# Fusion kernel: patch tiles cut across images, chunks of 384 tokens, patch rows normalised in PSUM, three periods

## Chip, core and metric

One core of one Trainium2 chip runs the whole program. The metric is the device time of one execution in microseconds (us). TensorE is called PE here and in the rows, VectorE DVE, ScalarE ACT, GpSimd POOL, and SyncE SP; SP does no arithmetic, it issues every DMA of this kernel.

## What is computed

64 images of 3 x 224 x 224 are cut into 14 x 14 patches of 16 x 16 pixels. Each patch is a row of 768 numbers that is normalised, multiplied into 256 columns and normalised again. 77 text rows are put behind the 196 patch rows of an image, so that an image has 273 tokens. An attention and a gated feed-forward layer follow, each with a residual.

```python
B, C, H, Wd = img.shape
x = img.reshape(B, C, H // PH, PH, Wd // PW, PW)
x = jnp.transpose(x, (0, 2, 4, 3, 5, 1))
x = x.reshape(B, -1, PH * PW * C)
x = _layernorm(x, ln1_g, ln1_b)
x = jnp.einsum('bnd,de->bne', x, W) + b
x = _layernorm(x, ln2_g, ln2_b)
...
h = jnp.concatenate([h, txt], axis=1)
h = h + _L0_attn_ref(_layernorm(h, axis=-1), L0_attn_Wq, L0_attn_bq, L0_attn_Wk, L0_attn_bk, L0_attn_Wv, L0_attn_bv, L0_attn_Wo, L0_attn_bo)
h = h + _L0_ffn_ref(_layernorm(h, axis=-1), L0_ffn_W_r, L0_ffn_W_k, L0_ffn_W_v, L0_ffn_mu_r, L0_ffn_mu_k)
...
return y.reshape(n, s, h, d).transpose(0, 2, 1, 3)
...
scores = jnp.einsum('nqhd,nkhd->nhqk', Q, K) * scale
attn = jax.nn.softmax(scores, axis=-1)
out = jnp.einsum('nhql,nlhd->nqhd', attn, V)
...
xr = mu_r * x + (1.0 - mu_r) * x_prev
xk = mu_k * x + (1.0 - mu_k) * x_prev
r = jax.nn.sigmoid(jnp.einsum('btc,dc->btd', xr, W_r))
k = jnp.einsum('btc,dc->btd', xk, W_k)
k_act = jnp.square(jax.nn.relu(k))
out = r * jnp.einsum('btc,dc->btd', k_act, W_v)
```

Because of the transpose ahead of it, the attention is one among the 16 heads of a single token: 16 x 16 scores for each token, and no token sees another.

## The kernel before, in words

The work has two grains. An **image** is loaded in two DMAs into xim (84 rows: two halves of a patch, three channels, 14 grid rows), copied by ACT into xcols so that a patch column lies together, transposed by PE in 14 pieces (the jobs x, L1106), and split from PSUM into a rounded part (xh, ACT, L951) and the rest (xl, DVE, L770), both in xT. PE multiplies xT by wtok in two halves of 98 rows with 18 matmuls of 258 columns each (the jobs tok, L1118). Column sums of squares (sq on ACT, ssq on DVE L765) go through two small matmuls against imask (the job stat, L1125) in a bank of their own. DVE then takes each half out of PSUM into y (yn, L786), and normalises it in SBUF: bn_stats and bn_aggr, hg (L800: y minus mean times g2b), h (L806: times rs2 plus b2b, into yh). POOL computes the two inverse roots with pow (L625, L609). SP copies yh into hc, which holds the token rows.

A **chunk** is 364 tokens, three to four images ("a quad"), so 48 chunks; its token tiles have 126, 126 and 112 rows. Per chunk: normalise (xn), transpose (xt, L1134), six products of 384 columns (qkv, L1026), a round trip through DRAM (qkv_dram) that brings q and k into qk and v into vrow, spreading of q (qplace, DVE L829) and of k (kspread, four ACT operations of 768 columns, L921) into block-diagonal operands, then scores (s, L1075), softmax, transposes (pt, L1083), the product with v (av, L1096), a second round trip (o_dram), ont (L1152), wo, normalise, zt (L1166), the mix with the token before (mix on DVE L872, mixh on ACT L1000, mixl on POOL L667), and the products k, r and val with their readers kr and rt (ACT, L1005, L1014) and rv (DVE, L878). DRAM rows 364 to 384 of a chunk are zeros, since attention handles 384 rows whatever is in them.

Everything is unrolled, and each engine runs its instructions in the order of one table, AT, of start steps, in which an image recurs every 3000 steps and a chunk every 4000, and all of it every 12000 (a quad):

```python
SLOT, IMG, QUAD = 4000, 3000, 12000
BANK = dict(x=[5, 7, 2], tok=[7, 2], stat=[5], xt=[6, 5], qkv=[4, 1, 6, 3, 4, 3], s=[0, 1], pt=[1, 4], av=[1, 6],
    ont=[1, 3], wo=[3, 6, 5], zt=[1, 6], k=[4, 0], r=[3, 6, 4], val=[0, 1, 3])
```

BANK says which of the eight PSUM banks a PE job writes. Before a job PE waits (turn) until the reader of the bank's last job is done. Every wait of SP stands in the one queue in which all its DMAs stand (helpers after, L284). Each product has six matmuls (three pairings of rounded part and rest, two halves of the depth), all counted under L1026.

Of the kernel before, what the change touches and what calls it, by code (L numbers as in the profile page):

```python
# [10 lines left out]

# [35 lines left out]
VROW = 5 * HD  # L50
# [1158 lines left out]
```

How the kernel before makes its waits and increments, by code:

```python
    def wait(self, eng, q, k, steps):  # L162
        eng.wait_ge(self.sem, q * (self.count * self.per) + (self.base + k * self.per + steps * self.unit))
# [1 line left out]
    def done(self, ins):  # L165
        ins.then_inc(self.sem, self.unit)
        return ins
# [9 lines left out]
    def wait(self, eng, q, k):  # L177
        back, i = divmod(k, len(self.pers))
        eng.wait_ge(self.sems[i], q * self.pers[i] + (2 + back) * self.pers[i] + self.pers[i])
# [267 lines left out]
            def load_rest():  # L448
# [4 lines left out]
                        sp.dma_start(dst, v.rearrange("(a e) -> a e", a=1).broadcast_to((128, E))).then_inc(raw_in, 16)  # L453
                    for n, w in enumerate(WEIGHTS):
                        sp.dma_start(rawsq[n], w.rearrange("(a p) e -> p a e", p=128)).then_inc(raw_in, 16)
                    for s, v in ((0, mu_k), (1, mu_r)):
                        sp.dma_start(mus[:, s, :], v.rearrange("(k p) -> p k", p=128)).then_inc(raw_in, 16)
                sp.wait_ge(prep_pool, 1)
                for c in range(CPQ):
                    sp.dma_start(qkv_dram[c, CT:CTP, :, :].rearrange("t i j -> t (i j)"), qkvt[0:CTP - CT, 0, :]).then_inc(raw_in, 16)
# [9 lines left out]
            def body(q):  # L470
# [10 lines left out]
                    for k in due(q, s, "txt", 0):  # L481
                        back, m = divmod(k, IPQ)
                        c = back * CPQ + text_pieces(m)[-1][2]
                        if q * IPQ + k == 0:
                            sp.wait_ge(prep_act, ACT_CLEAR)
                        after(xn_sb, q, c - CPQ, 3)
                        after(hb_sb, q, c - CPQ, 1)
```

## Time and profile before

| | |
|---|---|
| median of 3 runs | 1630.25 us (1625.87 to 1648.1) |
| profiled execution, first to last instruction | 1635.7 us |
| its mean granted PE clock | 0.968 of full speed |
| busy: PE, DVE, ACT, POOL | 1454.6, 1332.3, 1099.9, 973.6 us |
| DMA packets, bytes | 702658, 227.65 MB |

The page gives no other time for the profiled execution than its span. Busy time counts arithmetic only; SP's share is read from its own queue's rows below.

### The profile page before, as it was taken

What the parts mean: (1) busy time and instruction counts of PE and PEld (TensorE: products, weight loads), DVE (VectorE), ACT (ScalarE), POOL (GpSimd) and SP (SyncE); (2) the same over time, 40 slices, a digit from 0 to 9 for tenths busy, and PEclk for the clock granted to TensorE, in tenths of its full rate; (3) what the DMA queues carried; (4) which work ended last, traced back from release to release, by engine and by line L of the source; (5) the groups of instructions that cost most, each with busy time, mean ns of one, the idle gap of its engine ahead of it and who ended that gap; (6) DMA issues with size and microseconds to landing.
All of it is one profiled execution on the core that took longest, in us unless ns stands there. A gap on an engine that the chain in (4) does not pass through costs nothing. (4 is left out here: it accounts for less than half of the span.)

```text
span 1635.7 us, 53680 instructions
## 1 busy us (share of the span) xinstructions
PE 1454.6 (89%) x18762; PEld 1382.2 (85%) x18762; DVE 1332.3 (81%) x3075; ACT 1099.9 (67%) x2230; POOL 973.6 (60%) x1507
## 2 busy tenths in 40 slices
PE   4678899899999999999999999999999999998856
PEld 4677898898998898889898898998988988897756
DVE  5576888798988989898898888898898988888642
ACT  4455777677777776776777676777777776775543
POOL 2121566567656666666766765675675676576556
PEclk8798999999999999999999999999999999999988
DMA  4279979889877887888887896898898799887651
GB/s 121 59 141 138 141 147 150 125 159 157 143 157 141 147 155 143 150 137 165 149 140 157 151 141 127 167 157 141 152 154 140 151 159 140 156 151 118 131 74 37
DMA packets 702658, 227.65 MB, mean 139 GB/s; under 512 B 617470, under 2 KB 673854, under 8 KB 702394
## 3 DMA queue, kind: packets, MB, share of 16 engines
q1 hardware_dynamic: 702394, 224.23, 77.9%
q8 instruction: 153, 2.51, 0.8%
q14 instruction: 111, 0.91, 0.2%
HBM read 121.64 MB, written 89.64 MB: 129 GB/s over the span
## 5 line engine op out<-in xcount | busy, mean ns | idle before, releaser
L1026 PE MATMUL bank<-wqkv,xnT 128*126 128x384 f32 (+1 forms) x1728 | 354.2, 349 | 5.5 <-issue 5.5
L1118 PE MATMUL bank<-wtok,xT 128*98 128x258 f32 x2304 | 310.2, 290 | 12.0 <-DVE xT L770 11.4
L1026 PEld LDWEIGHTS bank<-wqkv,xnT 128*126 128x126 f32 (+1 forms) x1728 | 294.0, 185 | 18.3 <-issue 10.2
L1118 PEld LDWEIGHTS bank<-wtok,xT 128*98 128x98 f32 x2304 | 294.2, 171 | 14.6 <-DVE xT L770 13.2
L667 POOL TENSOR_TENSOR mixp<-mixf,mixp 128x364 fp32r<-128x364 f32 x192 | 185.2, 976 | 107.2 <-ACT mixp L1000 106.6
L921 ACT ACTIVATE arena<-qk,ymask 128x768 f32<-128x768 f32 x192 | 164.0, 926 | 97.6 <-DMA qk<-qkv_dram 97.6
L843 DVE TENSOR_TENSOR qkvt<-bank,bqkv 126x384 f32<-126x384 f32 (+1 forms) x288 | 154.0, 548 | 48.5 <-PE bank L1026 47.0
L654 POOL TENSOR_TENSOR dT<-zT 128x364 f32<-128x364 f32 x96 | 79.7, 851 | 153.9 <-ACT zT L994 153.9
L609 POOL TENSOR_TENSOR rs<-ve,small 126x3 f32<-126x3 f32 (+1 forms) x160 | 150.3, 940 | 12.5
L607 POOL TENSOR_TENSOR ve<-mv,small 126x3 f32<-126x3 f32 (+1 forms) x160 | 58.8, 368 | 158.8 <-DVE mv L865 104.0
L765 DVE TENSOR_REDUCE xs<-xim 84x14 f32<-84x1792 f32 x64 | 128.7, 2011 | 23.1 <-ACT xim L955 22.8
L872 DVE SCALAR_TENSOR_TENSOR mixf<-dT,mus,zT 128x364 f32<-128x364 f32 x192 | 125.8, 676 | 22.4 <-POOL zT L661 19.5
L943 ACT ACTIVATE xcols<-xim 84x640 f32<-84x640 f32 (+1 forms) x192 | 126.1, 693 | 25.4 <-DMA xim<-in_x 24.1
L1026 PE MATMUL bank<-woT,onT 128*126 128x256 f32 (+1 forms) x864 | 121.9, 287 | 12.4 <-DVE onT L849 12.1
L951 ACT ACTIVATE xT<-bank 128x420 fp32r<-128x420 f32 (+1 forms) x192 | 99.9, 532 | 44.5 <-PE bank L1106 44.2
L1026 PE MATMUL bank<-wrT,mixp 128*126 128x256 f32 (+1 forms) x864 | 124.9, 292 | 4.2 <-POOL mixp L667 3.7
L1026 PEld LDWEIGHTS bank<-woT,onT 128*126 128x126 f32 (+1 forms) x864 | 110.6, 186 | 17.7 <-DVE onT L849 16.9
L1026 PE MATMUL bank<-mixp,wkfT 128*128 128x364 f32 x576 | 123.5, 352 | 1.5 <-POOL mixp L667 1.4
L1075 PE MATMUL bank<-arena,qx 128*32 128x64 f32 x4608 | 83.0, 225 | 43.8 <-issue 43.8
L933 ACT ACTIVATE pt<-bank 64x384 f32<-64x384 f32 x192 | 93.0, 484 | 37.9 <-PE bank L1083 34.5
L682 POOL TENSOR_TENSOR h<-h,r 126x256 f32<-126x256 f32 x144 | 114.2, 807 | 6.1 <-DVE r L878 6.1
L1075 PEld LDWEIGHTS bank<-arena,qx 128*32 128x32 f32 x4608 | 74.1, 112 | 51.1 <-issue 47.4
(121 smaller groups left out, 3339.6 us busy)
## 6 DMA issues: line engine op xcount, KB each, us to landing
xim<-in_x SPq DMA_DIRECT2D x128, 294.0 KB
qk<-qkv_dram SPq DMA_DIRECT2D x48, 768.0 KB, 8.3
qkv_dram<-qkvt SPq DMA_DIRECT2D x96, 378.0 KB
arena<-qkv_dram SPq DMA_DIRECT2D x384, 48.0 KB, 3.9
qkv_dram<-qkvt SPq DMA_DIRECT2D x48, 336.0 KB
o_dram<-probs SPq DMA_DIRECT2D x288, 48.0 KB, 1.9
out<-h SPq DMA_DIRECT2D x96, 126.0 KB
on<-o_dram SPq DMA_DIRECT2D x64, 126.0 KB
```

The source lines that it names most:

```text
L609: done.done(P.tensor_tensor(rs[:, :], ve[:, :], powt[0:part, 0:ve.shape[1]], ALU.pow))
L667: mix_lo.done(P.tensor_tensor(mixp[:, w, 1, kk, :], mixf[:, kk, :], mixp[:, w, 0, kk, :].bitcast(F32), ALU.subtract))
L682: out_sb.done(P.tensor_tensor(dst, dst, r[0:rows, i, :], ALU.add))
L765: x_stats.done(V.tensor_reduce(xs[:, :], xim[:, :].rearrange("p (w q) -> p w q", q=128), AX.X, ALU.add))
L843: qkv_sb.done(V.tensor_tensor(qkvt[0:rows, i, NQ * half:NQ * half + NQ], place("qkv", job)[0:rows, 0:NQ], bqkv[0:rows, :, :].rearrange("p ...
L872: mix_sb.done(V.scalar_tensor_tensor(out=mixf[:, kk, :], in0=dT[:, kk, :], scalar=mus[:, w, kk:kk + 1], in1=zT[:, kk, 0:CT], op0=ALU.mult, ...
L921: kb_sb.done(A.activation(kb[:, :, yy, :], qk[:, :, HD:2 * HD], ACT.Copy, scale=ymask[:, yy:yy + 1]))
L943: x_cols.done(A.activation(xcols[:, 128 * w0:128 * w1].rearrange("p (w r q) -> p w r q", r=HALF, q=PS), xim[:, :].rearrange("p (r w q) -> ...
L951: x_hi.done(A.activation(xT[:, 0, :, w0:w1], src, ACT.Copy))
L1026: ins = mm(psum, left(a, k), right(b, k), start=t == 0, stop=t == len(terms) - 1)
L1075: ins = mm(place("s", part)[32 * j:32 * j + 32, col:col + 64], qx[:, g, :, :].rearrange("p x q -> p (x q)"), kb[:, g, :, :].rearrange("p y ...
L1118: ins = mm(place("tok", c)[0:PT, 0:E + 2], xT[:, a, i0:i0 + GRID // 2, :].rearrange("p i w -> p (i w)"), wtok[:, b, ch, :], start=t == 0, ...
```

## The change

- **Patch tiles.** The 896 grid rows of all images are one sequence, cut every 9 grid rows into 100 tiles of 126 patches. xT becomes a ring of 27 grid rows, so an image's 14 rows may wrap and are then written in two pieces (31 of 64 images: 95 pieces in all). A tile's matmuls are 18 as before. The matmuls on imask go into columns 258 to 271 of the tile's own bank, one set for each image that the tile touches (156 in all), and come ahead of the 18; stat is no job of its own any more.
- **Normalising in PSUM.** yn, hg and h read the tile's bank, yn and hg write back into it, and only h writes SBUF (yh, two buffers). The bank is held until h is done. tok takes banks 7 and 2 in turn, and x takes 5 and 0.
- **Chunks of 384 tokens** in three full tiles of 128 rows, 46 chunks for 17472 tokens; o_dram is a ring of eight images.
- **Attention in halves.** kb and qx hold half a chunk; kspread is two sets of four ACT operations, qplace two sets of two DVE copies, and the scores' second half waits for the second set, which waits for the first half's scores.
- **Mix.** It reads z from PSUM (the zt banks, held until mix is done). zT and d feed POOL as before; the row at an image's start is set by one POOL copy instead of a copy and a memset, with mu less 1 as the factor.
- **sq** writes into xcols in place, so the next xcols waits for ssq, and the next image's load waits only for xcols.
- **Three periods** in a new table: a chunk every 5376 steps, an image every 3822, a tile every 2457, and new banks for the rest.

The core of the diff:

```diff
-IPQ, CPQ = 4, 3
-QUADS = IMAGES // IPQ
-CHUNKS = QUADS * CPQ
-CT = IPQ * T // CPQ
-TOK = [(0, 126), (126, 126), (252, 112)]
-PT = 98
+TOKENS = IMAGES * T
+TT, TILES = 128, 3
+CT = TT * TILES
+CHUNKS = -(-TOKENS // CT)
+TROWS = 9
+PT = TROWS * GRID
+PTILES = -(-IMAGES * GRID // TROWS)
+RING = 3 * TROWS
...
-SLOT, IMG, QUAD = 4000, 3000, 12000
+SLOT = 5376
+IMG = SLOT * T // CT
+PTP = IMG * PT // PATCHES
...
+BANK = dict(x=[5, 0, 5], tok=[7, 2], xt=[3, 4], qkv=[6, 1, 6, 3, 3, 4], s=[3, 1], pt=[4, 1], av=[4, 6], ont=[3, 1], wo=[1, 3,
+    4], zt=[1, 6], k=[4, 6], r=[3, 4, 4], val=[3, 3, 4])
...
+                    y = place("tok", 0, t)[0:pr, 0:E]
...
+                    hg.done(V.scalar_tensor_tensor(out=y, in0=y, scalar=mv2[0:pr, 0:1], in1=g2b[0:pr, :], op0=ALU.subtract, op1=ALU.mult))
...
+                        mix_sb.done(V.scalar_tensor_tensor(out=mixf[:, kk, :], in0=dT[:, kk, :], scalar=mus[:, w, kk:kk + 1],
+                                                           in1=place("zt", kk, k)[:, 0:CT], op0=ALU.mult, op1=ALU.add))
...
+                        for k in due(s, "kspread", 4 * part + yy):
...
+                                qk_in.wait(act, k, 1)
+                                s_pe.wait(act, k - 1 + part, 1 if part else PARTS)
...
+                for t in due(s, "tok", 0):
+                    pr = patch_rows(t)
+                    m = patch_images(t)[-1]
+                    x_stats.wait(pe, m, 1)
+                    turn("tok", 0, t)
+                    for m in patch_images(t):
+                        i0 = TROWS * t - GRID * m + PAD
+                        mm(place("tok", 0, t)[0:pr, E + 2:E + 2 + GRID],
+                           imask[:, :, :].rearrange("p i w -> p (i w)")[:, GRID * i0:GRID * i0 + pr],
+                           xs[:, m % 2, :], start=m == patch_images(t)[0], stop=m == patch_images(t)[-1])
...
+                    terms = [(a, b, ch) for ch in range(KCH) for a, b in ((0, 0), (0, 1), (1, 0))]
+                    for n, (a, b, ch) in enumerate(terms):
+                        ins = mm(place("tok", 0, t)[0:pr, 0:E + 2], xT[:, a, ch, :, :].rearrange("p i w -> p (i w)")[:, r0:r0 + pr],
+                                 wtok[:, b, ch, :], start=n == 0, stop=n == len(terms) - 1)
```

Three places in the order of instructions. **PE, products r and val of one chunk, mid-program.** Here bank0 to bank7 are the PSUM banks, wrT marks an r product, wvfT a val product, wkfT a k product, wtok a patch tile. Before:

```order
L1118 MATMUL bank7<-wtok,xT 98x258 x18
L1026 MATMUL bank3<-wrT,mixp 126x256 x6
L1026 MATMUL bank6<-wrT,mixp 126x256 x6
L1118 MATMUL bank2<-wtok,xT 98x258 x18
L1026 MATMUL bank4<-wrT,mixp 112x256 x6
L1026 MATMUL bank0<-wvfT,kaT 126x256 x6
L1125 MATMUL bank5<-xs,imask 98x14 x2
L1026 MATMUL bank1<-wvfT,kaT 126x256 x6
L1026 MATMUL bank3<-wvfT,kaT 112x256 x6
```

Now, in the changed kernel, where L998 is the product helper and L1102 the tile:

```order
L998 MATMUL bank3<-wrT,mixp 128x256 x6
L1083 MATMUL bank5<-ident,xcols 128x84 x5
L998 MATMUL bank4<-wrT,mixp 128x256 x6
L998 MATMUL bank3<-wvfT,kaT 128x256 x6
L998 MATMUL bank4<-wrT,mixp 128x256 x6
L998 MATMUL bank3<-wvfT,kaT 128x256 x6
L1093 MATMUL bank7<-xs,imask 126x14 x2
L1102 MATMUL bank7<-wtok,xT 126x258 x18
L998 MATMUL bank4<-wvfT,kaT 128x256 x6
L1127 MATMUL bank3<-ident,on 128x128 x3
L1127 MATMUL bank1<-ident,on 128x128 x3
L998 MATMUL bank4<-mixp,wkfT 128x384 x6
```

Six products used five banks (3, 6, 4, 0, 1, 3); now they use two (3, 4, 3, 4, 3, 4) and are interleaved, and the next jobs, ont (ident,on) and k, take the same two banks.

**PE, scores and softmax of one chunk.** arena,qx marks scores, ident,probs the transposes pt, arena,pt2 the product with v. Before:

```order
L1026 MATMUL bank5<-woT,onT 112x256 x6
L1075 MATMUL bank0<-arena,qx 32x64 x24
L1075 MATMUL bank1<-arena,qx 32x64 x24
L1026 MATMUL bank6<-wqkv,xnT 126x384 x6
L1106 MATMUL bank5<-ident,xcols 128x84 x5
L1083 MATMUL bank1<-ident,probs 128x128 x3
L1083 MATMUL bank4<-ident,probs 128x128 x3
```

Now:

```order
L1051 MATMUL bank3<-arena,qx 32x64 x24
L998 MATMUL bank4<-woT,onT 128x256 x6
L1093 MATMUL bank2<-xs,imask 126x14 x2
L1102 MATMUL bank2<-wtok,xT 126x258 x18
L998 MATMUL bank6<-wqkv,xnT 128x384 x6
L1051 MATMUL bank1<-arena,qx 32x64 x24
L1059 MATMUL bank4<-ident,probs 128x128 x3
L998 MATMUL bank3<-wqkv,xnT 128x384 x6
```

The two halves of the scores stood side by side and now have one wo product and one qkv product (in some chunks a tile as well) between them.

**DVE, the patch rows.** bn marks the statistics, g2b marks hg, b2b marks h, bqkv the reader of a qkv product. Before:

```order
L741 TENSOR_REDUCE mx<-bank 128x24
L800 SCALAR_TENSOR_TENSOR y<-y,mv,g2b 98x256
L865 BN_AGGR mv<-bn 126x2
L741 TENSOR_REDUCE mx<-bank 128x24
L746 TENSOR_TENSOR probs<-bank,mx 128x384 x2
L860 BN_STATS bn<-h 112x6
L800 SCALAR_TENSOR_TENSOR y<-y,mv,g2b 98x256
L865 BN_AGGR mv<-bn 112x2
L806 SCALAR_TENSOR_TENSOR yh<-y,rs,b2b 98x256 x2
```

Now:

```order
L766 SCALAR_TENSOR_TENSOR bank<-bank,rstd,c0b 126x256
L770 BN_STATS bn<-bank 126x6
L817 TENSOR_TENSOR qkvt<-bank,bqkv 128x384
L776 BN_AGGR mv<-bn 126x2
L783 SCALAR_TENSOR_TENSOR bank<-bank,mv,g2b 126x256
L817 TENSOR_TENSOR qkvt<-bank,bqkv 128x384
L799 BN_STATS bn<-hc 128x6
L789 SCALAR_TENSOR_TENSOR yh<-bank,rs,b2b 126x256
```

Two halves of 98 rows with two SBUF inputs became one tile of 126 rows whose one input, and in hg the output too, is a bank.

Per program the DMAs number 1795 instead of 1792: 250 for yh to hc (224 before), 104 for text (96), 138 and 46 for q, k and v out and q, k in (144 and 48), 368 for v in (384), 424 for attention out (432), 200 back in (192), 137 for the output (144), 128 for the images (128).

## Rows read from the trace of the kernel before

**Rows 1.** The page, engines over the whole span: busy us, share, instructions.

```profile
PE 1454.6 (89%) x18762; PEld 1382.2 (85%) x18762; DVE 1332.3 (81%) x3075; ACT 1099.9 (67%) x2230; POOL 973.6 (60%) x1507
```

**Rows 2.** Busy time by stretch, and in the last columns PE clock, DMA share, GB/s.

```profile
0.00:150.00 150.00, 98.26 (x957) 91.47 (x958) 94.13 (x214) 71.32 (x127) 33.17 (x85) 0.85 0.56 111
...
250.00:1450.00 1200.00, 1122.02 (x14906) 1071.14 (x14910) 1047.40 (x2423) 863.50 (x1758) 771.46 (x1172) 0.99 0.84 148
...
1450.00:1636.00 186.00, 141.83 (x1734) 130.98 (x1723) 106.65 (x247) 95.98 (x206) 112.88 (x165) 0.92 0.56 99
```

**Rows 3.** Who waited for whom from 250 to 1450: us in total, times, longest.

```profile
PE bank L1075 <- issue: 26.9, 27, 2.9
PE bank L1152 <- DMA on<-o_dram: 24.9, 22, 2.5
PE bank L1026 <- DVE onT L849: 10.3, 16, 0.8
PE bank L1083 <- ACT probs L926: 5.8, 12, 0.5
```

**Rows 4.** The DMA queue's own waits from 250 to 1450, the five there are.

```profile
SPq L284 <- DVE probs L758: 38.5, 28, 1.8
SPq L284 <- DVE yh L806: 31.2, 13, 5.4
SPq L284 <- DVE qkvt L843: 13.8, 18, 1.9
SPq L284 <- DVE xs L765: 11.1, 16, 1.7
SPq L284 <- DMA o_dram<-probs: 1.5, 2, 1.3
```

**Rows 5.** Time line of SP, 717 to 733: start, duration, DMA, count.

```profile
717.37 0.39 SPq L514 DMA_DIRECT2D qk<-qkv_dram  x1
717.88 4.80 SPq L477 DMA_DIRECT2D xim<-in_x  x2
```

**Rows 6.** Line L921: min/median/max ns, first and last start.

```profile
L921 ACT ACTIVATE arena<-qk,ymask x192: 916/922/946, 101.0 to 1564.4; 128x768 f32<-128x768 f32 x192
```

**Rows 7.** Groups by line and shape: busy us, mean ns of one.

```profile
L1118 PE MATMUL bank<-wtok,xT 128*98 128x258 f32 x2304 | 310.2, 290 | 12.0 <-DVE xT L770 11.4 <-issue 0.6
L1026 PE MATMUL bank<-woT,onT 128*126 128x256 f32 x576 | 88.3, 291 | 12.4 <-DVE onT L849 12.1
L1026 PE MATMUL bank<-mixp,wkfT 128*128 128x364 f32 x576 | 123.5, 352 | 1.5 <-POOL mixp L667 1.4
L1106 PE MATMUL bank<-ident,xcols 84*128 84x84 f32 x896 | 96.0, 244 | 19.1 <-DVE y L774 6.3 <-DVE y L786 6.1 <-DVE xnT L833 2.9
L1125 PE MATMUL bank<-xs,imask 84*98 84x14 f32 x256 | 28.1, 222 | 0.7 <-issue 0.7
L800 DVE SCALAR_TENSOR_TENSOR y<-y,mv,g2b 98x256 f32<-98x256 f32 x128 | 116.2, 908 | 0.0
L926 ACT ACTIVATE probs<-probs 128x384 f32<-128x384 f32 x96 | 46.7, 521 | 65.6 <-DVE probs L746 65.5
```

**Rows 8.** Time line of PE, steady state, runs of 18 matmuls.

```profile
1494.33 2.29 PE L1026 MATMUL bank<-wvfT,kaT 128*126 128x256 f32 x18
...
814.72 2.31 PE L1118 MATMUL bank<-wtok,xT 128*98 128x258 f32 x18
```

**Rows 9.** Lines hg, yn and the POOL root: min/median/max ns.

```profile
L800 DVE SCALAR_TENSOR_TENSOR y<-y,mv,g2b x128: 447/476/2754, 41.9 to 1495.3; 98x256 f32<-98x256 f32 x128
L786 DVE SCALAR_TENSOR_TENSOR y<-bank,rstd,c0b x128: 463/474/485, 35.5 to 1485.5; 98x256 f32<-98x256 f32 x128
L609 POOL TENSOR_TENSOR rs<-ve,small x160: 693/972/1274, 42.5 to 1610.1; 126x3 f32<-126x3 f32 x96, 98x2 f32<-98x2 f32 x64
```

**Rows 10.** Time lines of PE and ACT, 804 to 812: r products and the last r's reader.

```profile
805.68 1.65 PE L1026 MATMUL bank<-wrT,mixp 128*126 128x256 f32 x12
...
810.80 0.36 ACT L1014 ACTIVATE r<-bank 112x256 f32<-112x256 f32 x1
```

More of the change, by code:

```diff
@@ L162, in wait @@
-    def wait(self, eng, q, k, steps):
-        eng.wait_ge(self.sem, q * (self.count * self.per) + (self.base + k * self.per + steps * self.unit))
+        self.per, self.unit = per, unit
+    def wait(self, eng, k, steps):
+        if k >= 0:
+            before = sum(self.per[:k]) if isinstance(self.per, list) else self.per * k
+            eng.wait_ge(self.sem, (before + steps) * self.unit)
     def done(self, ins):
@@ L883, in _ @@
+                for i in range(TILES):
+                    for k in due(s, "rv", i):
+                        val_pe.wait(dve, k, i + 1)
+                        r_tanh.wait(dve, k, i + 1)
+                        rv_sb.done(V.scalar_tensor_tensor(out=r[:, i, :], in0=r[:, i, :], scalar=1.0,
+                                                          in1=place("val", i, k)[:, 0:E], op0=ALU.add, op1=ALU.mult))
         @block.scalar
@@ new lines, in _ @@
+                for kk in range(2):
+                    for k in due(s, "xnh", kk):
+                        xn_pe.wait(act, k, kk + 1)
+                        qkv_pe.wait(act, k - 1, 6)
+                        xn_hi.done(A.activation(xnT[:, 0, kk, :], place("xt", kk, k)[:, 0:CT], ACT.Copy))
+                for kk in range(2):
+                    for k in due(s, "onh", kk):
+                        on_pe.wait(act, k, kk + 1)
+                        wo_pe.wait(act, k - 1, 3)
+                        on_hi.done(A.activation(onT[:, 0, kk, :], place("ont", kk, k)[:, 0:CT], ACT.Copy))
@@ L1018, in _ @@
+                for i in range(TILES):
+                    for k in due(s, "rt", i):
+                        r_pe.wait(act, k, i + 1)
+                        out_sb.wait(act, k - 1, 3)
+                        r_tanh.done(A.activation(r[:, i, :], place("r", i, k)[:, 0:E], ACT.Tanh, scale=0.5))
         @block.tensor
@@ L1093, in body @@
+                    for k in due(s, "av", part):
+                        pt_sb.wait(pe, k, 2 * part + 2)
+                        if part == 0:
+                            v_in.wait(pe, k, 8)
+                        turn("av", part, k)
+                        for row in range(UNITS):
+                            for j in range(4):
+                                b = PB * part + 4 * row + j
                                 for xx in range(2):
```

1369 lines of the change are left out of this document (648 added, 721 removed).

## Prediction

> **What bounds the kernel now.** I read the engine shares first [rows 1]: PE 89%, DVE 81%, ACT 67%, POOL 60%. A share over the whole span mixes fill, steady run and drain, so the next view is the busy time by stretch [rows 2]. From 250 to 1450 us PE is busy 1122.0 of 1200 us (93.5%), DVE 87%, ACT 72%, POOL 64%, and the 16 DMA engines 84%; the first 150 and last 186 us are much thinner. The chunk period comes from one line that runs in every chunk, the spread of k [rows 6]: first at 101.0, last at 1564.4, so (1564.4 - 101.0) / 47 = 31.14 us a chunk, with a head of 101.0 us and a tail of 1635.7 - 1564.4 = 71.3 us. 1200 us hold 38.5 such periods, so a period has 29.1 us of PE work and 2.0 us of PE idle. The waits [rows 3] tell which: 26.9 us before the scores (put down to "issue": their operands come from the spread, which came late), 24.9 us for the attention rows from DRAM, 10.3 and 5.8 us for short chains through DVE and ACT; together 67.9 of the 78 us.
>
> The view that one forgets is the DMA queue's own. SP waits only 96.1 us of the 1200 [rows 4], the five rows summed; the other 1103.9 us it is issuing or stepping through its queue, 28.6 us a chunk with 2.5 us of waits. A DMA issue is short in itself (0.39 us for q and k) but the two that come right behind it took 4.80 us [rows 5]: the queue pushes back. So **two** resources are over 90% taken, PE and SP. A change that makes PE's list shorter meets SP next.
>
> **The change, part by part: PE.** How much does a matmul cost with 126 rows instead of 98? The steady time line has runs of 18 of both kinds [rows 8]: 2.31 us for a half tile (98 rows, 258 columns), 2.29 us for a val job (126 and 112 rows, 256 columns). Rows are free, columns and count are paid.
> - Patch tiles: 310.2 / 2304 = 134.6 ns each [rows 7]; 2304 become 1800, 242.3 us, so -67.9 us. The dear end is the wo row with 126 rows, 88.3 / 576 = 153.3 ns, which gives 275.9 us, -34.3. I take the first, since the time line is the nearer row.
> - Matmuls on imask: 28.1 / 256 = 110 ns; two instructions for each of 156 sets, 312 in all, 34.3 us, +6.2.
> - Image transposes: 96.0 us, the same 896.
> - Products k: 123.5 us x 46/48 x 384/364 = 124.9, +1.4.
> - All else on PE is per chunk and per tile, whatever the rows: 1454.6 - 310.2 - 28.1 - 96.0 - 123.5 = 896.8 us, x 46/48 = 859.4, -37.4. This is the padding that leaves: attention handled 384 rows for 364 tokens already.
>
> Sum: -97.7 us (dear end -64.1), PE busy 1356.9 us, 29.50 us per chunk against 30.30 (1454.6 / 48). The steady 29.12 us becomes 28.35 us (29.05 at the dear end). With today's 2.0 us of idle the period would be 30.4 us (31.1).
>
> **DVE, ACT, POOL.** None sets the period, but they sit in PE's waits. hg takes 116.2 us for 128 [rows 7], though its median is 476 ns; single ones reach 2754 ns, while yn, which reads PSUM, never leaves 463 to 485 [rows 9]. With hg's input in a bank I expect 100 x 0.476 = 47.6 us, -68.6; 28 fewer yn and h save 28 x (0.474 + 0.476) = 26.6 more. Against that stand 93 extra pieces of xl and 88 extra qplace copies, at nothing if they only split the same columns and at 0.476 us each, 86 us, at worst. DVE ends between -95 and -9 us.
>
> Here two pages can be held against the rows. The Trainium skill, GPSIMD Engine Reference, section Specifications, says that GpSimd's SBUF interfaces are shared with VectorE and contended by DVE instructions with two SBUF inputs; the rows on hg and yn agree, and without that rule hg would go on costing 908 ns and the -68.6 us would be -25. The Trainium skill, VectorE: DVE Perf Modes, section on the TRN2 errata, speaks against the change: it prices a PSUM source at 120 cycles plus the columns and an SBUF source at 58, so 65 ns for each of 300 operations, about 20 us by the page; the rows show nothing of it, 474 ns from PSUM beside 476 from SBUF.
>
> ACT: 368 half spreads, at the 521 ns of an operation of 384 columns [rows 7], are 191.7 us, against 192 x 0.922 = 177.0 [rows 6], +14.7; 93 more xh pieces cost 0 to 0.521 us each, 48 us at most. POOL does five small operations for 36 more tiles, at most 36 x 5 x 0.972 = 175 us [rows 9], and has 36% to spare. All are covered by idle time of their own engines.
>
> **Waits that go and come.** The first scores now wait for four half spreads, 4 x (0.922 - 0.521) = 1.6 us less; this can clear the 0.7 us a chunk before the scores. The second scores wait for four more, 2.1 us, behind the first. Under them PE has one wo product (6 x 0.153 = 0.9 us) and one wider qkv product (over that): just about covered, and up to 2.1 us a chunk if ACT is late. PE's banks are tighter: six r and val products take turns in two banks, with one product between a bank's jobs at places. And a patch tile's whole group now waits behind the column sums (ssq) of its last image, with xt and the products of the chunk queued behind it on PE. I put 0.8 us a chunk of PE idle for all these beside the 2.0, less the 0.7 that goes: about 2.1, so 30.5 us from PE's side.
>
> **SP.** The DMAs are 1795 instead of 1792, over 46 periods instead of 48: 28.65 x 48/46 = 29.9 us of occupied queue a chunk. If its waits stay at 2.5 us the period is 32.4; if it runs without waiting, 29.9. I take 31.2 us, between PE's 30.5 and SP's 32.4, and nearer to PE's because SP's waits are for DVE, which gets lighter.
>
> **Head and tail.** Head: in the fill the image transposes of PE waited for the patch rows' DVE work in a shared bank and no longer do, [rows 7] 6.3 + 6.1 us; I take 5 us of it: 96 us (85 to 105). Tail: from the first spread of k to the output the old table has (33990 - 17070) / 4000 = 4.23 periods, the new one (50096 - 25900) / 5376 = 4.50: 71.3 x 4.50 / 4.23 = 75.9 us (66 to 80).
>
> **Sum:** 96 + 45 x 31.2 + 75.9 = 1575.9 us of span. The profiled execution, 1635.7 us, is 0.3% above the median of 1630.25; the same factor gives **1571 us**.
>
> **Rivals.**
> - *More gain.* The scores' wait and the DVE stalls go, and nothing comes for them: period 30.0 us, 96 + 1350 + 75.9 = 1521.9, 1517 us. For it: hg's long instances [rows 9] and the room given to the q and k DMA in the new table. Against: SP would have to run at 100% (29.9). Chance 0.13. By the page on GpSimd this gets likelier, as mix (two SBUF inputs before, one now) would be quicker as well.
> - *SP takes it all; no change.* The queue keeps 2.5 us of waits a chunk: 32.4 us, 96 + 1458 + 75.9 = 1629.9, 1624 us. For it: 92% taken now [rows 4, 5]. Against: the push-back is elastic, and q, k and v rows are 4% fewer. Chance 0.24.
> - *Banks; slower.* The reader of an r product can be late: in the trace the last r job ended at 807.33 and its tanh began at 810.80 [rows 10], 3.5 us behind other ACT work. That cost nothing with five banks. Now the val product that takes the same bank has one val product (0.76 us) ahead of it: 2.7 us a chunk if the lag stays, 31.2 + 2.7 = 33.9, 96 + 1525.5 + 75.9 = 1697.4, 1692 us. It decides from 2.05 us a chunk on. Against: ACT's order was laid anew, with the tanh near its product. Chance 0.13.
> - That the change doesn't do what it says I rule out: the lists show 1800 tile matmuls, 46 chunks and one-bank rows.
>
> **How the numbers follow.** Forecast 0.50, own range 1545 to 1597. A measurement of this kernel tells about 2% from no change, 1598 to 1663. Faster 0.50 + 0.13 = 0.63, within 2% 0.24, slower 0.13. The range leaves out the lower half of the best case and most of the slow one: 1520 to 1655.
>
> **What would show it.** Period from the first and last k spread near 31.2; PE busy near 1357 us and 18 tile matmuls in 2.3 us; hg near 476 ns with no long ones; SP's waits below 60 us per 1000; idle before r, val, ont or k on PE under 0.5 us a chunk. The prediction is wrong if PE waits for ACT's tanh or DVE's rv, if SP's waits on DVE grow, or if the drain exceeds 85 us.

## The result, and the profile after

The changed kernel takes 1822.53 us (median of 4 runs, 1815.13 to 1828.16) beside 1628.06 us for the kernel before on the same chip. The ratio is 1.114 with a 95% interval of 1.107 to 1.122: 11% slower, where I forecast 1571 us and put 0.13 on slower.

The page of the changed kernel, engine shares (answers to [rows 1]), the granted clock in 40 slices, and the DMA total:

```profile
PE 1468.3 (81%) x17678; PEld 1369.7 (75%) x17678; DVE 1232.8 (68%) x3109; ACT 1122.8 (62%) x2410; POOL 910.0 (50%) x1593
...
PEclk8687999999989988999898999999999998988988
...
DMA packets 677038, 225.57 MB, mean 124 GB/s; under 512 B 591853, under 2 KB 647980, under 8 KB 676780
```

Every share fell: no engine is nearer to its limit than before, and the DMA moves less. Something waits. The waits of the changed kernel from 250 to 1450 (us in total, times, longest), PE and SP, beside [rows 3] and [rows 4]:

```profile
PE bank L1127 <- DMA on<-o_dram: 129.9, 31, 8.5
PE bank L998 <- DVE r L854: 12.6, 9, 5.6
PE bank L1051 <- issue: 10.4, 17, 2.0
PE bank L1059 <- ACT probs L900: 8.7, 13, 1.4
...
SPq L292 <- DVE qkvt L817: 53.5, 22, 8.0
SPq L292 <- DVE yh L789: 48.8, 21, 5.4
SPq L292 <- DVE probs L735: 41.0, 23, 3.0
SPq L292 <- DMA o_dram<-probs: 13.3, 21, 2.7
```

One wait carries it: PE stands before ont until the attention rows come back from DRAM, 31 times in 32.9 chunk periods, 129.9 us where it was 24.9. The wait before the scores fell as hoped, 26.9 to 10.4. SP's own waits grew from 96.1 to 168.4 us (all six rows), where I had them shrink. The period, from the first and last spread of k, and the busy time of the stretch (columns as in [rows 2]):

```profile
L895 ACT ACTIVATE arena<-qk,ymask x368: 595/607/644, 113.0 to 1754.6; 128x384 f32<-128x384 f32 x184
```

```profile
250.00:1450.00 1200.00, 1009.96 (x12545) 943.72 (x12535) 854.73 (x2181) 786.43 (x1691) 638.44 (x1107) 0.93 0.71 132
```

(1754.6 - 113.0) / 45 = 36.48 us a chunk. PE is busy 84.2% of the stretch: 30.70 us of a period, 5.78 us idle. Head 113.0 us, tail 1822.1 - 1754.6 = 67.5 us. Against the forecast span of 1575.9 us the 246.2 us are 45 x (36.48 - 31.2) = 237.6 in the period, +17.0 in the head and -8.4 in the tail.

How does one such wait look? This is one of the longest (7.28 us; the longest is 8.5, the mean 129.9 / 31 = 4.2). The time line of the changed kernel, PE (start, duration, work, count, idle before it):

```profile
887.55 0.97 PE L1073 MATMUL bank<-arena,pt 128*32 128x68 f32 x48 [0.57 <-ACT pt L907]
...
899.02 0.46 PE L1083 MATMUL bank<-ident,xcols 84*128 84x84 f32 x4
906.75 1.54 PE L1127 MATMUL bank<-ident,on 128*128 128x128 f32 x6 [7.28 <-DMA on<-o_dram]
907.94 4.19 PE L998 MATMUL bank<-mixp,wkfT 128*128 128x384 f32 x12
```

and of its SP in the same microseconds:

```profile
889.65 4.05 SPq L504 DMA_DIRECT2D o_dram<-probs  x9
893.83 0.76 SPq L459 DMA_DIRECT2D xim<-in_x  x2
894.71 0.35 SPq L483 DMA_DIRECT2D qkv_dram<-qkvt  x1
895.18 0.37 SPq L523 DMA_DIRECT2D out<-h  x1
895.87 4.45 SPq L514 DMA_DIRECT2D on<-o_dram  x4
```

Read the two together. The value product of chunk k+1 ends on PE at 888.52. DVE divides (the last osb ends at 889.49), SP issues the writes of the rows (889.65 to 893.70) and four other DMAs, and issues the reads of chunk k from 895.87 to 900.32. The last rows have landed when PE starts at 906.75. That chain takes 18.2 us, and PE has work of its own for 11.0 of them, up to 899.48. In the kernel before, at one of its longest waits, the same chain took 16.2 us (923.56 to 939.76), and PE had work for all but 2.46.

One place proves little, so here are the means over every start of ont from 250 to 1450 us (38 in the kernel before, 32 in the changed one), in us, taken from the time lines; the runs e1, e8, e11 and e12 are told below:

| | value product's end to ont | PE busy in it | to the first read's issue | first read's issue to ont |
|---|---|---|---|---|
| before | 13.8 | 12.9 | 8.6 | 5.2 |
| changed | 15.4 | 10.7 | 8.7 | 6.8 |
| e1 | 14.7 | 10.7 | 8.0 | 6.7 |
| e12 | 15.2 | 10.7 | 8.5 | 6.6 |
| e8 | 12.3 | 10.8 | 8.3 before it | 20.5 |
| e11 | 18.6 | 13.0 | 9.8 | 8.8 |

So the mean loop is 15.4 us against 10.7 us of work. Compared with the kernel before, the work that covers it is 2.2 us less and the loop 1.6 us longer; up to the issue of the reads nothing has changed, and the 1.6 us lie behind it.

### The profile page after: what moved, and what is told of

Same layout as the page of the kernel before. It is cut to its first block and busy times, and to the rows that moved or that the text cites. A ratio compares the mean times of both kernels' runs of the same rounds, so it can differ in the third digit from the quotient of the medians.

```text
span 1822.1 us, 51616 instructions
## 1 busy us (share of the span) xinstructions
PE 1468.3 (81%) x17678; PEld 1369.7 (75%) x17678; DVE 1232.8 (68%) x3109; ACT 1122.8 (62%) x2410; POOL 910.0 (50%) x1593
## 3 DMA queue, kind: packets, MB, share of 16 engines
q8 instruction: 144, 2.36, 0.6%
## 5 line engine op out<-in xcount | busy, mean ns | idle before, releaser
L998 PE MATMUL bank<-wqkv,xnT 128*128 128x384 f32 x1656 | 337.0, 347 | 2.0 <-ACT dT L979 1.6
L998 PEld LDWEIGHTS bank<-wqkv,xnT 128*128 128x128 f32 x1656 | 285.0, 192 | 7.1 <-issue 2.8
L1102 PE MATMUL bank<-wtok,xT 128*126 128x258 f32 (+1 forms) x1800 | 253.4, 297 | 0.0
L637 POOL TENSOR_TENSOR mixp<-mixf,mixp 128x384 fp32r<-128x384 f32 x184 | 184.8, 1012 | 101.2 <-ACT mixp L974 100.6
L1102 PEld LDWEIGHTS bank<-wtok,xT 128*126 128x126 f32 (+1 forms) x1800 | 234.9, 198 | 0.0
L895 ACT ACTIVATE arena<-qk,ymask 128x384 f32<-128x384 f32 x368 | 196.9, 610 | 44.1 <-PE bank L1051 39.8
L1127 PE MATMUL bank<-ident,on 128*128 128x128 f32 x276 | 61.2, 379 | 195.5 <-DMA on<-o_dram 193.3
L817 DVE TENSOR_TENSOR qkvt<-bank,bqkv 128x384 f32<-128x384 f32 x276 | 148.9, 546 | 33.9 <-PE bank L998 33.6
L998 PE MATMUL bank<-mixp,wkfT 128*128 128x384 f32 x552 | 153.7, 442 | 0.7 <-DVE r L854 0.7
L916 ACT ACTIVATE xcols<-xim 84x640 f32<-84x640 f32 (+1 forms) x192 | 130.3, 693 | 26.4 <-DVE xs L743 18.6
L581 POOL TENSOR_TENSOR rs<-ve,small 126x1 f32<-126x1 f32 (+2 forms) x192 | 134.0, 698 | 15.0
L998 PE MATMUL bank<-wvfT,kaT 128*128 128x256 f32 x828 | 121.3, 290 | 20.2 <-DVE r L854 18.2
L998 PEld LDWEIGHTS bank<-mixp,wkfT 128*128 128x128 f32 x552 | 136.1, 267 | 1.0 <-POOL mixp L637 0.9
```

The source lines that it names most:

```text
L581: done.done(P.tensor_tensor(rs[0:pr, :], ve[0:pr, :], powt[0:pr, 0:ve.shape[1]], ALU.pow))
L637: mix_lo.done(P.tensor_tensor(mixp[:, w, 1, kk, :], mixf[:, kk, :], mixp[:, w, 0, kk, :].bitcast(F32), ALU.subtract))
L817: qkv_sb.done(V.tensor_tensor(qkvt[:, i, NQ * half:NQ * half + NQ], place("qkv", job, k)[:, 0:NQ], bqkv[:, :, :].rearrange("p i j -> p (i ...
L895: kb_sb.done(A.activation(kb[:, :, yy, :].rearrange("p (a u) k -> p a u k", u=UNITS), qk[:, :, HD:2 * HD].rearrange("p (a u) k -> p a u k" ...
L916: x_cols.done(A.activation(xcols[:, 128 * w0:128 * w1].rearrange("p (w r q) -> p w r q", r=HALF, q=PS), xim[:, :].rearrange("p (r w q) -> ...
L998: ins = mm(psum, left(a, k), right(b, k), start=t == 0, stop=t == len(terms) - 1)
```

## Experiments

Several theories stood at the start; the two that matter most are of the loop "value product, osb, writes, reads, ont": that the round trip of the data through DRAM binds, and that the halved clock behind the wait makes it expensive. In e1 to e4 theory A is the round trip, B that SP's queue is full, C tight banks; from e5 on C is the reads' place in SP's queue, and D a want of slack everywhere. Times are of one execution unless a ratio is given; the kernel before ran at 1628 to 1639 us beside them. Waits are those from 250 to 1450.

### e1: other rows

```diff
-                    after_all(o_out, k)
-                    if place_of(T * chunk_images(k)[-1] + T - 1)[0] > k:
-                        after_all(o_out, k + 1)
...
-                        src = o_dram[m % OIMAGES, :, :, :].rearrange("q t d -> (q t d)").rearrange("(r e) -> r e", e=E)
-                        on_in.done(sp.dma_start(on[p:p + rows, i, :], src[r0:r0 + rows, :]))
+                        src = txt.rearrange("b t e -> (b t) e")
+                        lo = (T * m + r0) % 4096
+                        on_in.done(sp.dma_start(on[p:p + rows, i, :], src[lo:lo + rows, :]))
```

> The changed kernel, but the attention rows (on) are read from the text input instead of o_dram, and SP no longer waits for the DMAs of this and the next chunk that write o_dram; every DMA is still issued, the output is not the reference's from the second residual on. Theory A (the round trip from the product with v of chunk k+1 to ont of chunk k takes about 15.5 us and PE has only 10 to 13 us of work between the two in its order): the idle before ont (397 us in the profile, both rows of PE) falls under 40 us, the chunk period falls from 36.5 to 31 us, total about 1575 us, and PE's busy time falls by some 90 us since the clock stays up. Theory B (SP's queue is the bound, the rival of the prediction): the number of DMAs is the same, so the period stays over 34 us, total over 1720 us. Theory C (tight PSUM banks): the idle moves to r, val, ont and k behind ACT and DVE, period over 33 us.

Measured: 1788.63 us. The reads depend on no write any more, and the wait stays: `on<-in_txt` 111.7 us, 31 times. So the need for the newest rows is worth 34 us of 194, and the theory of the round trip falls as the main cause (it had 1575 us). The time is over theory B's 1720, as it would be for anything else in SP's queue. What had not changed was where the reads stand: in SP's one queue, behind the nine writes that wait for the value product.

### e2: a period later

```diff
+LATER = ("o_in", "ont", "onh", "onl", "wo", "h2", ..., "val", "rv", "add", "out")
+AT.update({kind: [a + SLOT for a in AT[kind]] for kind in LATER})
```

hb gets a fourth slot, and xn lies over probs for the room.

> The changed kernel with everything from o_in to the output one whole chunk period (5376 steps) later, so that each engine's order inside a period and the banks stay, but PE has 28 us more work between av of chunk k+1 and ont of chunk k. hb gets a fourth slot, and xn lies in the memory of probs to make room. The output is the reference's. Theory A: the wait before ont goes away, the period is 31 to 31.5 us, and the drain is 20 to 31 us longer: 113 + 45 x 31.2 + 92 = about 1609 us, faster than the changed kernel by 11% and than the kernel before by 1%. Theory B: period over 34 us, total over 1750 us. Theory C: over 33 us, over 1700 us.

Measured: 1810.48 us, ratio 1.107 (1.099 to 1.114). The rows read were written a whole period before, and PE still waited 117.1 us for them, 30 times. The shift by exactly one period leaves every queue's order as it was. It says the same as e1, now with the reference's computation. PE's own work between a value product and the next ont is also as it was, 10.7 us in the mean.

### e3: other places of writes and reads

```diff
-o_out=[28315], o_in=[34008]
+o_out=[27965], o_in=[33345]
```

> The changed kernel with two numbers of the table: o_out at 27965 instead of 28315 and o_in at 33345 instead of 34008, so that SP sends the attention out right behind osb, ahead of other DMAs, and stands ready for it. Theory A: the chain from av to ont gets 2 to 2.5 us shorter and the period with it, total 1710 to 1740 us. Theory B: no change, since SP issues as much as before, 1815 to 1830 us. A third outcome: SP stands longer at o_in for the landing, and what is queued behind it (q and k in) comes late: no gain or a loss, 1820 to 1860 us.

Measured: 1917.92 us, worse even than the third outcome had it (1820 to 1860). The wait for `on` fell to 75.7 us, but the reads are now the next thing in SP's queue behind the writes, where they wait at its head for the writes' landing (45.9 us), and the rows of q, k and v behind them go late: SP then waited 119.5 us for their landing, ACT 73.0 us for q and k, PE 68.6 us before the scores. A gain for one reader was paid by the next in the queue.

### e4: busy PE

```diff
+                        turn("ont", kk, k)
+                        if kk == 0:
+                            for n in range(32):
+                                mm(place("ont", 0, k)[:, 384:512], wmat["woT"][:, 0, 0, 0:128], wqkv[:, 0, 0, 0:128],
+                                   start=True, stop=True)
                         on_in.wait(pe, k, ROW_DMAS[k])
-                        turn("ont", kk, k)
```

> The changed kernel with 32 extra matmuls of 128 columns a chunk on PE, ahead of its wait for the attention rows, into unused columns of ont's bank; they fill some 2 to 3 us of the wait. Theory A with a share of the clock (the stall of 4 us lets the granted clock fall, mean 0.93 in the steady part, and the k products behind it then take twice as long, which lies in the same loop): clock over 0.97, period shorter by 1 to 2.4 us, total 1715 to 1775 us. If the clock has no part in it: 1815 to 1850 us.

Measured: 1811.91 us, with 32.1 us of wait left beside the added matmuls, and a granted clock over the span 0.946 instead of 0.912. The mean of the k products behind the wait came down from 442 to 392 ns; k products and ont transposes together take 36 us less. The time came down by 11 us, which is less than the 13 us by which the changed kernel's own four runs differ. So filling the wait doesn't mend the kernel. It doesn't price the clock either: only a part of the lower clock went, and the 1472 added matmuls were busy 175.8 us, not all of it in waits, so that the mean loop grew from 15.4 to 15.9 us. Work at the lower clock stands behind ont and ahead of the next value product, where nothing covers it; e8 gives a better price for it.

### e5 and e6: the reads ahead of the writes

e1 and e2 with the reads ahead of the writes in SP's queue: o_in=[34008] becomes [33574] in both.

> Edit: e1 again (the attention's rows of a chunk are read from text rows of the input instead of the ones just written, so the output is not the reference's), and their four issues stand in SP's queue ahead of the nine o_dram issues of the chunk after, not behind them (o_in at table step 33574 instead of 34008). Nothing else moves. In e1 the wait for `on` stayed (111.7 us in 250 to 1450) though the data did not depend on anything; there the four issues at 922.67 stood behind hc<-yh (wait of 5.6 us for DVE), nine o_dram issues (4.16 us) and two more. Theory C (SP's queue: the reads are late because they stand behind issues that wait for the attention's result): they come at least 4.16 + 0.35 + 0.36 = 4.9 us earlier, the mean wait of 111.7 / 31 = 3.6 us goes, the wait for `on` falls below 30 us in that stretch, and the time falls by 3 to 3.6 us a chunk from 1788 us, to 1620 to 1660. Theory D (the stretch of PE's work is short for another reason, and the wait only stands where another would): the wait for `on` goes, but others (s issue, r from DVE, probs) take its place and the time stays above 1740.

> Edit: e2 again (the whole group from the attention's projection to the end one period later, computing the same as the reference), with the reads of the attention's rows ahead of the nine o_dram issues in SP's queue (o_in at 33574 instead of 34008, both a period later). In e2 the rows read had been written a period before, and still the wait for `on` was 117.1 us (30 times) and the time 1810. Theory C (SP's queue): the wait falls below 30 us in 250 to 1450, the time to 1640 to 1690 (a chunk of the pipeline's tail more than e5). Theory D: above 1750. If the write's flight to memory and back were what counts, e2 would have shown it already; it can give nothing here.

Measured: 1820.28 us, and 1840.82 us (ratio 1.127, 1.121 to 1.132). Both misses. The wait for `on` went as expected, to 10.7 and 14.9 us, and the time did not. SP's waits in e6:

```profile
SPq L296 <- PE bank L1148: 119.4, 30, 10.9
SPq L296 <- DMA qkv_dram<-qkvt: 63.7, 30, 4.4
SPq L296 <- DVE qkvt L823: 31.4, 16, 5.5
```

L1148 is zt of the chunk before: `on` is a single buffer that also holds z, so its reads must wait until PE has transposed z. Ahead of the writes they do that at the head of SP's queue, up to 10.9 us, and hold up the writes and the rows of q, k and v. In e5 DVE waited 87.9 and ACT 114.1 us for q and k. By their numbers both runs came out as theory D had it: the wait for `on` went and others took its place, above all the one before the scores (98.2 us in e5, 62.2 in e6), and both times are above 1740. SP's rows tell where these come from: the queue blocks on whichever late thing stands at its head. Whether that is all of it, e5 and e6 can't say; e8 and e9 were made for it.

### e7: less cover in the kernel before

The kernel before, group LATER moved by -350 steps.

> Edit: the kernel before, with nothing changed but the place in the table of the group from o_in to the output: 350 steps (2.0 us of a 31.1 us period) earlier. Every instruction and every shape is as before; the work of PE between the attention's value product of the chunk after and the projection's first transposes shrinks from 15.5 to 17.2 us by about 2 us. The wait for `on` was 24.9 us in 250 to 1450. Theory C (the loop value product, osb, SP's queue, reads, transposes has a fixed length which the work between must cover): the wait grows by up to 38.5 x 2.0 = 77 us, to between 50 and 100 us, and the time to 1655 to 1720. Theory D: the wait for `on` may grow but the time stays within 1.5% of 1628.

Measured: 1865.76 us, slower than I gave it, and not for the reason I gave: the wait for `on` is in none of the seven largest of PE, whose idle time is spread over seven readers at 16 to 27 us each, while SP waits 121.9, 103.8 and 83.8 us for qkvt, xs and probs. Moving a group against the rest reorders DVE, ACT and POOL too. The run shows how sensitive the old table is (14% for 350 steps of 4000), and says nothing about the loop. It warns too: a place moved can cost as much without the loop, so that a longer time alone proves nothing; the row that carries it has to be the loop's.

### e8 and e9: two buffers, and reads where nothing late stands ahead

```diff
-        on = sb("on", [TT, TILES, E])
+        on = sb("on", [TT, 2, TILES, E])
...
-                    after(z_pe, k - 1, 2)
-                    after(on_pe, k - 1, 2)
+                    after(z_pe, k - 2, 2)
+                    after(on_pe, k - 2, 2)
...
-o_in=[34008]
+o_in=[31000]
```

e8 is e2 with these lines, e9 is e1 with them. For the room e8 also takes a narrower row of v in SBUF (VROW), one buffer for the statistics of both norms (bn3, bn4) and a corner of r for mx, with the waits that these need.

> Edit: e2 (the projection's group one period later, computing the same as the reference) with two buffers for `on` instead of one, so that the reads of a chunk's attention rows need neither the newest o_dram writes nor the transposes of z of the chunk before, and their four issues put where SP has nothing late ahead of them (o_in at table step 31000, both values a period later: after arena's eight issues, some 1800 steps before o_out). e6 showed what one buffer does: the reads ahead of the o_dram issues waited 119.4 us for the transposes of z, and the queries and keys behind them in SP's queue came late. Theory C' (what costs the time is the reads' place in SP's one queue: behind o_out they wait for the value product, ahead of it for the buffer): now they wait for nothing; PE's waits for `on` are below 10 us in 250 to 1450, SP's own waits below 120, and the time is 1610 to 1690. Theory D (the new order of the table is short of slack everywhere, and any stall removed is followed by the next one: s, probs, r): PE idles 150 us or more in 250 to 1450 for other reasons and the time stays above 1740.

> Edit: e1 (the attention's rows of a chunk are read from text rows of the input, so the output is not the reference's; the group from the projection on stands where the changed kernel has it) with two buffers for `on` and the four issues at step 31000, and xn laid over probs for the room. Theory C': as for e8 but without the extra period in the pipeline's tail: waits for `on` below 10 us, time 1580 to 1660. Theory D: above 1740. If e8 and e9 part by more than 60 us, it is the place of the group against its banks that counts, not SP's queue.

Measured: e8 1662.17 us, ratio 1.018 (1.010 to 1.026); e9 1688.23 us, 28 us above its range. e8 is 160 us faster than the changed kernel and has its computation, tiles, chunks, halves and banks. The waits of PE and SP in e8, with no row of `on` among the larger ones, and its stretch:

```profile
PE bank L1009 <- DVE r L862: 30.8, 15, 8.4
PE bank L1062 <- issue: 14.5, 17, 3.1
PE bank L1070 <- ACT probs L908: 10.5, 15, 1.4
...
SPq L296 <- DMA qkv_dram<-qkvt: 67.7, 34, 4.1
SPq L296 <- DVE probs L743: 26.7, 16, 2.8
SPq L296 <- DVE yh L797: 21.8, 16, 2.7
SPq L296 <- DVE qkvt L825: 17.4, 6, 5.0
```

```profile
250.00:1450.00 1200.00, 1091.05 (x13966) 1017.11 (x13967) 947.48 (x2427) 872.43 (x1888) 713.13 (x1234) 0.98 0.73 147
```

```profile
L903 ACT ACTIVATE arena<-qk,ymask x368: 592/603/646, 109.9 to 1575.5; 128x384 f32<-128x384 f32 x184
```

SP waits 136.1 us in its five rows, more than the 120 I allowed. Its period is (1575.5 - 109.9) / 45 = 32.57 us, 3.91 less than the changed kernel's. Of these, 2.82 us are idle of PE that went (5.78 to 2.96), and 1.09 us are busy time (30.70 to 29.61), about what the k products and ont transposes had lost to the lower clock, 57 us in 46 chunks. SP's waits for DVE's qkvt, yh and probs fell from 143.3 to 65.9 us with DVE's work as it was: they had been the same loop seen from SP. e8 issues as many DMAs as the changed kernel, so theory B of e1, that SP's queue is full, falls too. Where those waits were, SP now waits 67.7 us for the landing of qkvt's rows (3.8 before).

In e8 the reads have time. Their issues take 1.84 us a chunk in the median and 7.96 at worst, and PE needs the rows 20.5 us after the first issue, so even the worst does no harm. The worst one on e8's SP (of the eight reads of v, the first row shows five):

```profile
899.40 5.65 SPq L503 DMA_DIRECT2D arena<-qkv_dram  x5
905.31 1.43 SPq L480 DMA_DIRECT2D hc<-yh  x2
907.05 7.96 SPq L518 DMA_DIRECT2D on<-o_dram  x5
```

### e10: two more places

```diff
-qk_in=[23298], st3=[17696, 17851, 17879], mv3=[17898, 17910, 17923], rstd3=[18181]
+qk_in=[23450], st3=[18046, 18201, 18229], mv3=[18248, 18260, 18273], rstd3=[18480]
```

> Edit: e8 with two more places moved, for what is left there: the statistics of LN3 350 steps later (st3, mv3, rstd3, up to the step before xn), since DVE stood 42.6 us in 250 to 1450 waiting for hc's rows at the head of its queue and PE 30.8 us behind it for DVE's r; and the transfer of queries and keys 152 steps later, since SP stood 67.7 us in front of it for the landing of qkvt's last rows. Computes the same as the reference. Of PE's idle of 109 us in 1200 some 30 can go: a period of 31.6 to 32.3 us instead of 32.57, 1620 to 1650 us. If the waits only move, 1655 to 1670. With that it would stand within 1% of the kernel before (1628 to 1635), and the rest of the forecast gain is in PE's own longer work and in the extra period of the pipeline.

Measured: 1663.92 us, ratio 1.018 (1.013 to 1.023), as foreseen if the waits only move: the wait for DVE's r is 34.5 us (30.8), DVE's for hc 35.9 (42.6). No version beats the kernel before.

### e11: late reads in the kernel before

```diff
-o_out=[18883], o_in=[23572]
+o_out=[18883], o_in=[23972]
```

> Edit: the kernel before, with one step moved: the reads of the attention's rows 400 table steps later (o_in 23572 to 23972, 3.1 us of a 31.1 us period), which puts them behind the transfer of queries and keys in SP's queue. All shapes, all other places as before. It makes in the kernel before what the change made in its own way: reads that land late against PE's transposes. They now land about 6.5 us after their issue with a wait of 24.9 us in all; 3.1 us later and behind a transfer of 8.3 us they come 3 to 9 us later. Theory C': the wait for `on` grows to between 90 and 250 us in 250 to 1450 and the time to 1720 to 1900. If the loop has slack elsewhere (theory D: only the whole balance of the table counts): below 1680.

Measured: 1895.14 us. One step of the kernel before moved, 3.1 us of its period, and 256 us are lost; its waits on PE are the changed kernel's, only more so:

```profile
PE bank L1152 <- DMA on<-o_dram: 176.6, 32, 6.4
PE bank L1026 <- issue: 3.6, 2, 2.7
```

Nearly all of PE's idle (1200 - 1013.95 = 186.1 us) is this wait. Of the loop, the cover is as in the kernel before (13.0 us) and the length is 18.6 us instead of 13.8: the reads are issued later, their issues take 5.8 us in the median instead of 1.6, and the rows land later.

### e12: the buffer alone

e8's second buffer and xn over probs in the changed kernel, no step moved.

> Edit: the changed kernel with e8's second buffer for `on` (and xn laid over probs for its room) and nothing moved: the reads stand where the change put them, behind the o_dram writes of the chunk after, computing the same as the reference. It takes from e8 what e8 needed for room, so that the gain of e8 (1662 against 1823) can be put down to the reads' place. Theory C' (their place in SP's queue against the value product and the writes): the wait for `on` stays at 110 to 140 us in 250 to 1450 and the time at 1800 to 1840. Rival (the single buffer itself held the reads, by waiting for the transposes of z): below 1740.

Measured: 1805.92 us, `on` 124.1 us, 33 times. By one run, the buffer gives 17 us by itself, little more than the spread of the changed kernel's runs (13 us). The other 144 us of e8's gain come with the reads' place together with e2's later group, without which the rows aren't there yet; that group alone gave 12 us (e2), and the small edits for e8's room are in it as well. e1 and e9 show the place without the later group: 1788.63 to 1688.23 us, with a second buffer in e9, and xn over probs for its room, as the only other difference.

## Why the prediction was wrong

**Where it failed: "Waits that go and come".** I listed what would newly wait (second scores, banks, ssq) and kept "the 2.0" of today's idle, in which the 24.9 us for the attention rows stood [rows 3], as if a wait stayed as long as it was. It did not: in the mean the loop has 10.7 us of PE work over it and is 15.4 us long, where the old had 12.9 over 13.8. The tables had told the cover before any run: from the last value product of the next chunk to ont are 24528 - 4000 - 18232 = 2296 of 4000 steps in the old one, 0.57 of a period, and 35251 - 5376 - 27546 = 2329 of 5376 in the new one, 0.43. A chunk of 384 tokens also ends inside an image, so its rows need the next chunk's writes in nearly every chunk, 45 of 46, where it was two of three. I forecast 2.1 us of PE idle and it is 5.8. e11 shows in the kernel before what late reads do to this loop; e1, e9, e12 and e8 show that with the reads out of their place behind the writes most of the loss is gone, while the need for the newest rows is worth 34 us. That less cover alone would do it, with the reads left where they are, is argued from the means and was not tried.

**"SP's waits are for DVE, which gets lighter".** DVE did get lighter, 1332.3 to 1232.8 us, 99.5 us less, 5 us beyond my -95 to -9. SP's waits grew from 96.1 to 168.4. They were not DVE's load: DVE's osb and qkvt wait for PE, PE for the reads, the reads for SP. A wait in a loop says nothing of the engine named in it. The period of 31.2 "between PE's 30.5 and SP's 32.4" was thus a mean of two bounds where the loop was a third. Nor is the time that I called taken a fixed amount of work: by the same count (1200 us less SP's waits) it is 31.4 us a chunk in the changed kernel and 28.9 in e8, where I had 29.9.

**Why slower had 0.13.** The one rival that was slower rested on banks. That the kernel is slower was no merit of it: it priced 2.7 us a chunk for r, and PE waited 12.6 + 4.3 us in 32.9 periods for r's readers, 0.5 us a chunk. With the loop out of the way, in e8, it is 30.8 + 4.2 us in 36.8 periods, 0.95 us a chunk. Of my signs of being wrong, SP's waits on DVE did grow, from 94.6 to 143.3 us, and for a cause that I hadn't listed.

**PE busy, -97.7 us.** It is +13.7 in the changed kernel. Some of that is work at the lower clock behind the wait: the k products are 153.7 us against 112.9 in e8, the ont transposes 61.2 against 44.6, together 57 us. e8, at a clock of 0.98 in the stretch, gives 1427.6 us, -27. Its groups:

```profile
L1113 PE MATMUL bank<-wtok,xT 128*126 128x258 f32 (+1 forms) x1800 | 254.4, 298 | 0.0
L1009 PE MATMUL bank<-woT,onT 128*128 128x256 f32 x828 | 129.8, 297 | 5.3 <-DVE xnT L816 5.3
L1009 PE MATMUL bank<-wrT,mixp 128*128 128x256 f32 x828 | 128.6, 298 | 6.2 <-POOL mixp L642 3.4 <-ACT r L999 2.7
L1009 PE MATMUL bank<-wvfT,kaT 128*128 128x256 f32 x828 | 126.7, 298 | 34.3 <-DVE r L862 32.5 <-ACT r L999 1.4
L1104 PE MATMUL bank<-xs,imask 84*126 84x14 f32 (+1 forms) x312 | 46.7, 251 | 11.6 <-DVE xs L751 11.5
```

A group's busy time counts the tail of its last matmul, which lies under the next group: the groups sum to 1607 us for PE's 1427.6 (before: 1621 for 1454.6). Group by group, my forecast sums to 1516 us for 1356.9, and e8 is 91 us above it; 20 of these are more such overlap, 71 are PE's own time. By groups: tiles +12.1 (254.4 for 242.3, between my two ends), imask +12.4, image transposes +7.6, k -12.0, and "all else per chunk and per tile, whatever the rows" +71. In that, the products wo, r and val are the largest: 385.1 us, where 362.7 x 46/48 = 347.6 was forecast. Six of them alone are busy mostly 0.85 to 0.98 us, twelve 1.54 to 1.67 and eighteen 2.29, and in the new order more stand alone: from 900 to 1000 us 9 of 19 runs in the kernel before, from 950 to 1000 us 13 of 15 in e8. But that is mostly the tail counted more often. From the start of such a run to the start of the next job, where PE doesn't idle between them, six take 0.74 us in the median and twelve 1.50 in the kernel before, and 0.79 and 1.52 in e8 (250 to 1450 us). Standing alone costs next to nothing; that six take 0.05 us more in e8 stays unexplained. For a tile's 18 the same measure gives 2.15 us with 98 rows and 2.24 with 126, so "rows are free" was 4% too cheap. wqkv came out at 337.9 for 339.4. With e8's PE at 29.6 us a period, instead of 28.35, my 2.1 us of idle would have given 31.7.

**Right.** hg takes 416/484/495 ns (minimum, median, maximum; [rows 9] had 447/476/2754), so the term of -68.6 us holds; a tile's 18 matmuls with 126 rows take 2.38 to 2.41 us, near the forecast 2.3; the scores' wait fell; DVE's size, but for the 5 us. Both rules that were weighed are answered by the same row. The long instances are gone with one SBUF input, which is what the Trainium skill, GPSIMD Engine Reference, section Specifications, would have. And the 65 ns that the Trainium skill, VectorE: DVE Perf Modes, section on the TRN2 errata, adds for a PSUM source are not in it: 484 ns from PSUM with 126 rows beside 476 from SBUF with 98, 8 ns.

The tail (75.9) is 67.5, the head (96) is 113.0: the first 150 us have a clock of 0.78 against 0.85 [rows 2] and 92.1 us of PE work against 98.3; why, was not tried.

**What stays open.** Whether the changed kernel would do with ont at its old share of a period from the value product. Why the reads take 1.6 us longer from issue to ont. Why e9, without the extra period, is 26 us slower than e8 (its SP waits 74.0 us for qkvt's rows, 67.7 in e8; its DVE 50.0 us for hc, 42.6 in e8). How much the second scores' half cost alone was not tried. e8 against the kernel before, 32.57 us a period against 31.14, is 1.4 us: PE idle 3.0 against 2.0 and busy 29.6 against 29.1; the head and tail are 190.8 us against 172.3, with a group that runs a period later.

## What to carry to other kernels

A wait of 25 us in 1200 can be the visible end of a loop that is nearly closed. Before a table is changed, follow each DRAM round trip from the PE job that starts it to the PE job that needs it, add up every issue ahead of the read in the DMA queue, and compare that with the PE work between the two jobs in the new order; here the old trace had 13.8 us of loop under 12.9 us of work, and the tables cut the distance from 0.57 to 0.43 of a period. A read behind a write in one queue inherits the write's wait even when it needs none of its data; give it a second buffer and a place where nothing late is ahead, and do both at once, as either alone only moved the block (e6, e12).

## What the hardware showed that I had not expected

- Issuing the same reads can take very different times. In the kernel before the four issues of `on` take 1.44 to 2.71 us (38 chunks), right ahead of the transfer of q and k. In e11, where they stand right behind it, the four take 5.06 to 8.44 us in every one of 33 chunks. The sizes are the same, so what stands ahead in the queue counts. But it isn't settled by the neighbours alone: in the changed kernel the 4.45 us shown above is the longest of 32, behind nine writes and two image loads as in the kernel before, and the median is 1.89; in e8 the 7.96 us is the longest of 36.
- In the 7.28 us without work PE's granted clock fell to 0.50, the level of 1.2 GHz, and stayed there for 6 us of work: twelve k products took 4.19 us (2.36 in e8 at 964.67), and the transposes 418 ns each instead of 273 (the median in e8). Windows of the changed kernel show the fall and the return (columns as in [rows 2]):

```profile
902.00:904.00 2.00, 0.00 (x0) 0.00 (x0) 0.00 (x0) 0.00 (x0) 0.22 (x1) 0.59 1.32 199
...
910.00:912.00 2.00, 2.00 (x8) 1.90 (x8) 0.90 (x3) 1.75 (x2) 0.78 (x3) 0.50 0.65 87
...
914.00:916.00 2.00, 2.00 (x19) 2.00 (x18) 1.82 (x4) 0.55 (x3) 0.83 (x1) 1.00 1.58 58
```

- The lower clock is a consequence of the waits and a cost of its own: some 57 us of longer k products and transposes. e4 gave back 36 of them and gained 11 us with its added matmuls; e8 is free of all 57, along with the waits.
